# DLRM tower with gathered embeddings: where the upper layers stand in TensorE's order, who adds the row numbers, when the late weights are loaded

## The reference

```
e = stack(tbl_f[ids[:, f]])                        # 2048 x 26 x 64
x = layer_norm(dense @ Wd.T)                       # 2048 x 128
y = layer_norm(e @ Ws.T)                           # 2048 x 26 x 128
y = layer_norm(einsum('bne,pn->bep', y, Wsi))      # 2048 x 128 x 32
T = concat([x, y^T])                               # 33 vectors of 128
Zflat = lower triangle of T @ T^T                  # 528
z = layer_norm(Zflat @ Wl.T) * mask(384)           # 2048 x 512
h = relu([z, dense] @ W_top1 + b1)                 # 512
h = relu(h @ W_top2 + b2)                          # 256
out = h @ W_top3                                   # 2048 x 1
```

## Time and profile before

| What | Value |
| --- | --- |
| median of 3 runs | 572.98 us |
| the profiled execution: span from first to last instruction | 572.2 us |
| TensorE matmuls busy | 509.5 us (89%) |
| VectorE busy | 400.8 us (70%) |
| ScalarE busy | 280.8 us (49%) |
| GpSimd busy | 400.9 us (70%) |
| mean granted TensorE clock | 0.967 |
| gathers, L530 | 416, 398.4 us busy, 958 ns each, 126.8 us idle in front of them |
| y_var, L409 | 64, 1220 ns each |
| projection, L631 | 64 pairs, 662 ns a record |

### The profile page before, as it was taken

The page is one execution under the profiler, slowest core; times in us unless marked ns, Lnnn a source line. Parts: engine busy times, 40 slices in busy tenths (PEclk is TensorE's granted clock), DMA queues, the critical chain, the costliest instruction groups (busy, mean ns, idle before and its releaser), DMA issues.

```text
span 572.2 us, 17022 instructions
## 1 busy us (share of the span) xinstructions
PE 509.5 (89%) x6783; PEld 396.8 (69%) x6783; DVE 400.8 (70%) x707; ACT 280.8 (49%) x727; POOL 400.9 (70%) x423
## 2 busy tenths in 40 slices
PE   1768759899999999999999999999999999898887
PEld 1644438677868677777778687778677777777665
DVE  3747666786778878677878786878878776777720
ACT  0514553454636555455545454646455455545433
POOL 5777777777777777777777777777777777777000
PEclk9958886999999999999999999999999999999999
DMA  7711113131212213131313131222213131313020
GB/s 266 281 28 29 25 29 90 27 91 28 82 38 67 51 33 87 27 93 28 91 28 93 27 91 29 78 41 67 54 39 80 27 90 29 91 27 91 5 65 1
DMA packets 28704, 36.39 MB, mean 64 GB/s; under 512 B 10731, under 2 KB 19379, under 8 KB 28113
## 3 DMA queue, kind: packets, MB, share of 16 engines
q0 software_dynamic: 13408, 13.81, 12.6%
q1 hardware_dynamic: 15218, 21.50, 11.0%
HBM read 26.09 MB, written 9.18 MB: 62 GB/s over the span
## 4 chain that ended last, share of the span: by engine, by line
PE 22%; POOL 22%; DVE 22%; issue 19%; ACT 9%; DMA 4%; SPq 1%; DVEq 0%; ACTq 0%
POOL rows L530 22%; PE bank_z L661 7%; DVE y_var L409 5%; PE bank_d L689 4%; DVE y L399 4%; DVE r_vec L425 4%; PE bank_z L644 4%; ACT y_sq L813 3%; DVE bank_z L417 2%; ACT y_std L819 2%; DMA wsi_b<-in_wsi_b 2%; DVE scaled L364 2%; PE bank_b L631 2%; PE bank_z L604 1%; ACT h L893 1%
## 5 line engine op out<-in xcount | busy, mean ns | idle before, releaser
L530 POOL DMA_INDIRECT rows<-in_table,ids_all x416 | 398.4, 958 | 126.8 <-issue 125.9
L409 DVE TENSOR_REDUCE y_var<-y_sq 128x32 f32<-128x1024 f32 x64 | 78.1, 1220 | 45.3 <-ACT y_sq L813 45.3
L813 ACT ACTIVATE y_sq<-y 128x512 f32<-128x512 f32 x128 | 80.3, 631 | 36.7 <-DVE y L399 36.4
L631 PE MATMUL bank_b<-mixed,gs_row 64*128 64x512 f32 x128 | 74.4, 662 | 19.8 <-ACT mixed L842 19.6
L644 PEld LDWEIGHTS bank_z<-r_vec 128*32 128x32 f32 x4096 | 47.8, 111 | 59.8 <-issue 58.0
L621 PE MATMUL bank_a<-wsi_b,scaled 128*128 128x192 f32 (+3 forms) x512 | 84.0, 309 | 2.1 <-DVE scaled L389 2.0
L425 DVE TENSOR_TENSOR r_vec<-y,bank_z 128x512 f32<-128x512 f32 x128 | 82.3, 684 | 2.2
L621 PEld LDWEIGHTS bank_a<-wsi_b,scaled 128*128 128x128 f32 x512 | 78.2, 195 | 3.2 <-DVE scaled L389 3.2
L661 PE MATMUL bank_z<-wl,zd 128*128 128x512 f32 x160 | 74.7, 614 | 1.2 <-DMA zd<-zx 1.2
L835 ACT ACTIVATE row_std<-row_var,eps 128x8 f32<-128x8 f32 (+1 forms) x64 | 19.2, 300 | 113.6 <-DVE row_var L373 89.3
L631 PE MATMUL bank_c<-mixed,gs_row 64*128 64x512 f32 x128 | 74.4, 662 | 0.0
(11 more groups left out here) (111 smaller groups left out, 609.4 us busy)
## 6 DMA issues: line engine op xcount, KB each, us to landing
zx<-zs SPq DMA_DIRECT2D x15, 560.0 KB, 3.8
rows<-in_table,ids_all POOLq DMA_INDIRECT x416
dense_t<-in_dense_t SPq DMA_DIRECT2D x1, 2048.0 KB, 8.5
wl<-in_wl SPq DMA_DIRECT2D x1, 1280.0 KB
w<-in_w SPq DMA_DIRECT2D x1, 1280.0 KB, 16.3
wsi_b<-in_wsi_b SPq DMA_DIRECT2D x1, 1248.0 KB, 11.5
zd<-zx SPq DMA_DIRECT2D x15, 80.0 KB
zd<-zx SPq DMA_DIRECT2D x15, 70.0 KB
```

What stands on the lines that cost most here:

```text
L409: v.tensor_reduce(y_var[:, k % BANKS, :], y_sq[:, k % 2, :, :].rearrange("e a (s p) -> e (a s) p", p=PROJ), AX_X, ALU.add).then_inc(y_var_ ...
L530: nc.gpsimd.indirect_dma_start(rows[t % 2][:, c, D * blk:D * (blk + 1)], None, io["table"], bass.IndirectOffsetOnAxis(ap=ids_all[:, n:n + ...
L631: pe.matmul(bank_y[blk][:], gs_row[half, :], mixed[half, k % 2, :], start=True, stop=True)\
L813: nc.scalar.activation(y_sq[:, k % 2, blk, :], y[:, k % 2, blk, :], ACT.Square).then_inc(y_squared, 1)
```

## The change

In TensorE's loop `upper(w)` moves from the end of the step to the place between `gram_product(w+1)` and `project(w)`; only `turn_z`, which stood in `upper`, stays at the end of its step. ids and first row numbers come in one load, and VectorE adds them in two pieces (tile 0, then tiles 1 to 15) where GpSimd added them in one; the first gathers wait for the first piece, all later ones for the second. The load of `wl` waits for `prep` at "x_row0", the loads of `w1`, `w2` and `w3` for "end". The masks get a semaphore of their own, and the three users of `wl` (`fold`, `scale_linear`, `last_step_weights`) wait for its load.

```diff
--- before.py
+++ after.py
@@ -110,8 +110,8 @@
         ident = sb("ident", [P, P])
         ones = sb("ones", [P, P])
         eps = sb("eps", [P, 1])
-        ids_all = sb("ids_all", [P, TILES * 2 * CHUNKS], I32)
-        row_base = sb("row_base", [P, 2 * CHUNKS], I32)
+        ids_based = sb("ids_based", [P, (TILES + 1) * 2 * CHUNKS], I32)
+        row_base, ids_all = ids_based[:, 0:2 * CHUNKS], ids_based[:, 2 * CHUNKS:]
         ws_t = sb("ws_t", [P, E])
         gs_row = sb("gs_row", [P, E])
         ws_e = sb("ws_e", [P, P])
@@ -172,8 +172,9 @@
         x_r = sb("x_r", [P, TILES])
         out_row = sb("out_row", [1, B])
 
-        s_ids, s_small, s_wsi, s_wl, s_dense, s_top = (
-            sem(n) for n in ("ids_loaded", "small_loaded", "wsi_loaded", "wl_loaded", "dense_loaded", "top_loaded"))
+        s_ids, s_small, s_wsi, s_masks, s_wl, s_dense, s_top = (
+            sem(n) for n in ("ids_loaded", "small_loaded", "wsi_loaded", "masks_loaded", "wl_loaded", "dense_loaded",
+                             "top_loaded"))
 
         gathered = [[sem(f"gathered_{parity}_{g}") for g in range(len(GROUPS))] for parity in ("even", "odd")]
         ids_ready = sem("ids_ready")
@@ -258,6 +259,16 @@
                 dve.wait_ge(prep, count[0])
 
             v = nc.vector
+
+            def add_row_base(first, end):
+                v.tensor_tensor(ids_all[:, 2 * CHUNKS * first:2 * CHUNKS * end].rearrange("p (t n) -> p t n", t=end - first),
+                                ids_all[:, 2 * CHUNKS * first:2 * CHUNKS * end].rearrange("p (t n) -> p t n", t=end - first),
+                                row_base.rearrange("p (o n) -> p o n", o=1).broadcast_to([P, end - first, 2 * CHUNKS]),
+                                ALU.add).then_inc(ids_ready, 1)
+
+            dve.wait_ge(s_ids, 16)
+            add_row_base(0, 1)
+            add_row_base(1, TILES)
             step(v.memset(eps[:], EPS))
             step(v.memset(ones[:], 1.0), "constants")
             dve.wait_ge(s_small, 16 * 7)
@@ -322,7 +333,7 @@
                 finish_x(j)
 
 
-            dve.wait_ge(s_wl, 16 * 3)
+            dve.wait_ge(s_masks, 16 * 2)
             bq = col["bsi_q"].rearrange("p (t o) -> p t o", o=1)
             fw = fold_w[:, :, 0:64]
             step(v.tensor_tensor(fw, mask_a[:].rearrange("p (o n) -> p o n", o=1).broadcast_to([P, STEPS, 64]),
@@ -334,6 +345,7 @@
 
             def last_step_weights():
 
+                dve.wait_ge(s_wl, 16)
                 dve.wait_ge(fold_done, 1)
                 last = wl[:, 0, :]
                 step(v.tensor_scalar(last, last, col["gsi_q"][:, 0:1], None, ALU.mult))
@@ -472,19 +484,20 @@
 
         @block.sync
         def _(sp):
-            for dst, src in ((ids_all, "ids"), (row_base, "row_base")):
-                sp.dma_start(dst[:], io[src]).then_inc(s_ids, 16)
+            sp.dma_start(ids_based[:], io["ids_based"]).then_inc(s_ids, 16)
             for dst, src in ((ws_t, "ws_t"), (gs_row, "gs_row"), (ident, "ident"), (cols, "cols"),
                              (wd_t, "wd_t"), (wsi_n, "wsi_n"), (bs_row, "bs_row")):
                 sp.dma_start(dst[:], io[src]).then_inc(s_small, 16)
             sp.dma_start(dense_t[:], io["dense_t"]).then_inc(s_dense, 16)
             sp.dma_start(wsi_b[:], io["wsi_b"]).then_inc(s_wsi, 16)
-            for dst, src in ((wl, "wl"), (mask_a, "mask_a"), (mask_b, "mask_b")):
-                sp.dma_start(dst[:], io[src]).then_inc(s_wl, 16)
+            for dst, src in ((mask_a, "mask_a"), (mask_b, "mask_b")):
+                sp.dma_start(dst[:], io[src]).then_inc(s_masks, 16)
+            sp.wait_ge(prep, prep_at["x_row0"])
+            sp.dma_start(wl[:], io["wl"]).then_inc(s_wl, 16)
+            sp.wait_ge(prep, prep_at["end"])
             for dst, src in ((w1, "w1"), (w2, "w2"), (w3, "w3")):
                 sp.dma_start(dst[:], io[src]).then_inc(s_top, 16)
 
-            sp.wait_ge(prep, prep_at["zd"])
             for t in range(TILES - 1):
                 sp.wait_ge(zs_kept, BANKS * (t + 1))
                 if t:
@@ -513,15 +526,12 @@
 
         @block.gpsimd
         def _(pool):
-            pool.wait_ge(s_ids, 32)
-            nc.gpsimd.tensor_tensor(ids_all[:].rearrange("p (t n) -> p t n", t=TILES),
-                                    ids_all[:].rearrange("p (t n) -> p t n", t=TILES),
-                                    row_base[:].rearrange("p (o n) -> p o n", o=1).broadcast_to([P, TILES, 2 * CHUNKS]),
-                                    ALU.add).then_inc(ids_ready, 1)
-            pool.wait_ge(ids_ready, 1)
-
             def gather(k):
                 t, q = divmod(k, BANKS)
+                if k == 0:
+                    pool.wait_ge(ids_ready, 1)
+                if k == 1:
+                    pool.wait_ge(ids_ready, 2)
                 if t >= 2:
                     pool.wait_ge(rows_scaled, k - 2 * BANKS + 1)
                 for c in GROUPS[q]:
@@ -574,6 +584,7 @@
 
             def fold():
 
+                pe.wait_ge(s_wl, 16)
                 for t in range(STEPS):
                     mm = pe.matmul(bank_l[0:65, :], fold_w[:, t, :], wl[:, t, :], start=(t == 0), stop=(t == STEPS - 1))
                 mm.then_inc(fold_done, 1)
@@ -728,7 +739,6 @@
                 if q == 3 and tile >= 1:
                     if tile < TILES - 1:
                         first_dense(tile - 1)
-                        turn_z(tile - 1)
                     else:
                         linear(tile - 1, range(STEPS))
 
@@ -756,6 +766,7 @@
                     mix(w)
                 if ahead:
                     gram_product(w + 1)
+                upper(w)
                 if new:
                     project(w)
                 if old:
@@ -766,7 +777,8 @@
                     fold()
                 if w == 4:
                     fold_bl()
-                upper(w)
+                if w % BANKS == 3 and 1 <= w // BANKS < TILES - 1:
+                    turn_z(w // BANKS - 1)
             end()
 
 
@@ -794,6 +806,7 @@
             def scale_linear(steps):
 
                 if steps[0] == 1:
+                    act.wait_ge(s_wl, 16)
                     act.wait_ge(fold_done, 1)
                 for t in steps:
                     nc.scalar.activation(wl[:, t, :], wl[:, t, :], ACT.Copy, scale=col["gsi_q"][:, t:t + 1],
@@ -1028,8 +1041,8 @@
     ws = np.asarray(x["L0_rec_Ws"])
     arrays = {
         "table": np.concatenate(tables),
-        "ids": ids.reshape(P, -1),
-        "row_base": np.repeat(first_row[feature].T, 2, axis=1).astype(np.int32),
+        "ids_based": np.concatenate([np.repeat(first_row[feature].T, 2, axis=1).astype(np.int32), ids.reshape(P, -1)],
+                                    axis=1),
         "ident": np.eye(P, dtype=f32),
         "ws_t": np.concatenate([ws.T, ws.T]),
         "gs_row": np.broadcast_to(np.asarray(x["L0_rec_gs"]), (P, E)),
```

## The result

The changed kernel took 627.96 us (median of four runs, 626.94 to 628.04), the kernel before 573.35 in the four runs beside it: ratio 1.0944, 95% interval 1.0922 to 1.0967. The forecast was 629.6, in a range of 616 to 642. The profiled execution took 628.0 us and has a span of 626.2.

A forecast was written before the change was run, and what follows sets the result against it. Gathers bound the old kernel, with TensorE close; the new order's loop of waits was to set the time. Its steps reach 598.8, plus 31.0 of tail, less 1.0 at the start, plus 0.8 to the median: 629.6 us, range 616 to 642.

The forecast's parts named there:

- The bound of the old order: Gathers set the old kernel's end at 32.8 us a tile, with TensorE's chain at 30.6 nearly equal.
- The ring: Loop of waits through the engines between successive keep_y(w, 0); with upper products inside, 34.7 us a tile sets the time.
- q = 1: Second of a tile's four steps, q = 0 to 3; its period with second_layer before the projection was forecast at 8.3 us.
- the slack: Spare time in the old loop of waits, which held no upper product; an upper product's full time was to be added.
- The 0.3 us for the copies before the first square: Copies of z and x on ScalarE delay the first square; 0.3 us added to the period after each q = 0 step.
- The start: Before the loop, fewer early loads let wsi_b arrive sooner: gain between nothing and 5.7 us, taken as 1.0.
- a loss of up to 0.5 us: First gather slowed beside VectorE's second addition with two SBUF inputs, losing up to 0.5 of the 1.1 us gained.
- The sum: Step periods added from step 5 at 97.85 put the last keep_y at 598.8; with 31.0 after it, 629.8 us.
- The tail: From the last keep_y to the end: 31.0 us, not shortened by the earlier linear of tile 14.
- (a): Rival: the loop of waits has unseen slack and gathers still set the end, 576 us; chance 0.08.
- (b): Rival: faster, gathers start 1.1 us earlier and stay the bound, 571.9 us; chance 0.04.
- (c): Rival: TensorE's clock falls, its lower level held a tenth of the time, 656 us; chance 0.06.

The follow-up runs named there:

- e7: e1 with first_layer alone moved between gram and projection on TensorE: 589.96 us, ratio 1.024 to the kernel before.
- e1: The changed kernel with TensorE's old order put back, row numbers on VectorE and late weight loads kept: 574.26 us, ratio 0.9964 to the kernel before.
- e11: e1 run once more, unchanged, beside e9 and e10: 573.03 us, ratio 0.9977 to the kernel before.
- e6: e1 with third_layer alone moved between gram and projection on TensorE: 575.11 us, ratio 0.9987 to the kernel before.
- e8: e1 with VectorE's one subtraction over wsi_b cut into six pieces: 572.96 us, ratio 0.9948 to the kernel before.
- e9: e1 with third_layer between gram and projection and VectorE's subtraction over wsi_b in six pieces: 573.23 us, ratio 0.9984 to the kernel before.
- e10: e1 with all weights loaded at the start, so only the row numbers on VectorE remain of the change: 572.97 us, ratio 0.9977 to the kernel before.
- e2: The kernel before with TensorE's new order alone, loads and row numbers as before: 628.49 us, ratio 1.0886 to the kernel before.
- e3: The changed kernel with ScalarE's copy of the turned rows put before the second square: 605.01 us, ratio 1.0503 to the kernel before.
- e5: The changed kernel with the upper products between mix and gram, not between gram and projection: 605.91 us, ratio 1.0523 to the kernel before.
- e4: The changed kernel with linear alone put back at the end of its step: 612.58 us, ratio 1.065 to the kernel before.

## Why the prediction was right, point by point

**The bound of the old order.** Two limits lay close. e7 shows it: 1.3 us a tile more, and the end is TensorE's, no longer the gathers'. e1 and e11 show the other side: TensorE's chain is 5 us ahead at step 7 (108.33 and 108.62) and has no lead left at step 59 (512.86 and 512.41, against 512.97). In the traces of the kernel before and of e1, e6, e8, e9, e10 and e11 the end comes 43.0 to 44.1 us behind the start of the last gather. That spread is about as large as the differences between them, so a shift of the end by a few tenths of a us can't be traced to the gathers.

**The ring.** Right in place and size. Forecast 8.4, 8.3, 10.6 and 7.3; measured 8.29, 7.93 to 8.30, 10.74 and 7.27. e2 shows that the order alone does it, e3 that ScalarE's order closes the ring, e6 and e7 that a piece costs only what is over the slack. The 0.3 us for the copies before the first square shows in q = 1 in one of three or four tiles; I had put it in each. A tile as forecast, 34.7, is 0.2 over the mean of 34.50, 2.6 us over 13 tiles; over an undisturbed tile, 34.3, it is 0.4. The fall of the clock in tile 7, told below, hides some of it.

**The start.** Forecast a gain of 1.0, measured 0.73 at the first transposition. The gathers start 0.87 earlier, forecast 1.1, both within their bounds. The first gather, for which I had a loss of up to 0.5 us beside the second addition, took 1.20 us where it was 1.17. The gain of 0.73, though, compares two traces. The first transposition starts at 32.60 to 33.61, 32.99 on the mean, in the nine with row numbers on VectorE and the subtraction in one piece, and at 33.33 and 33.52 in the two with the old loads: some 0.4 us, less than the traces differ among themselves. The rule of the Trainium skill ("DMA: Bandwidth & Descriptors", section "Queues, rings and completion order") gave half a microsecond less gain than my 1.0; 0.73 lies between, and the means are nearer to it. e10 speaks for the rule: with `wl` and the rest queued behind it `wsi_b` came no later than in e1_loads and e11.

**The sum.** y of step 5 was forecast at 97.85 - 1.0 = 96.85 and came at 96.66; step 7 at 113.8 and 113.41; step 59 at 564.9 and 561.89; step 63 at 597.8 and 594.51. The tail was 31.0 and came as 31.7, and the runs' median lay 1.8 and not 0.8 above the span. The 0.8 was a misreading: I took the span of one execution from the median of others, and in every run the time is 1.8 to 1.9 us over the span of the same run. The errors partly cancel, which is luck: 0.4 too much up to step 7, 2.6 in the 13 tiles and 0.3 in tile 15, against 0.7 and 1.0 too little in the tail and above the span, 1.6 us in all.

**The tail** grew by 0.7, which I had no term for. In the last tile TensorE has nothing to do between the interaction of step 62 and that of step 63. From the changed kernel's timeline of TensorE:

```profile
600.13 1.16 PE L655 MATMUL bank_z<-r_vec 128*32 128x35 f32 x64 [4.95 <-DVE r_vec L437]
601.22 3.78 PE L691 MATMUL bank_a<-dense_t,w 128*128 128x128 f32 x16
...
608.96 4.57 PE L672 MATMUL bank_z<-wl,zd 128*128 128x512 f32 x10
```

After 4.95 us without work the interaction takes 1.16 us and `first_dense` 3.78, where it took 2.05 in the earlier trace rows: the granted clock was 0.50 from 600 to 605. e2_order, with the same order and the same wait of 4.95 us, shows that this is nearly the whole of it: there `first_dense` took 3.10, 0.68 less, and the tail was 30.9. In the kernel before `linear` of tile 14 stood in this gap. `linear` of the last tile then started behind `first_layer`, without a wait for its z, where it had waited 1.16 us for it before.

**What was wrong.** GpSimd did not wait for scaled rows from tile 12: only two gathers, at 245.57 and 522.07, were released by `scale_rows`, and both started after the usual 0.3 us. VectorE waits for the projection at q = 0, 1 and 2 (1.1, 0.9 and 3.7 us), but not at q = 3, where its own work is as long as the ring; I had said 1.5 to 6 us in each step. TensorE waits 0.3 to 1.7 us in front of gram, where I had 0.6 to 1.7. None was a term of the sum.

**The rivals.** (a) and (b) fall with e2. (c), a lower clock, happened in a small way:

```profile
297.85 1.33 PE L621 MATMUL bank_z<-gram,rows_t 128*128 128x128 f32 x6 [1.41 <-ACT rows_t L840]
298.98 3.23 PE L713 MATMUL bank_z<-h,w 128*128 128x128 f32 x16
```

In tile 7 the second layer took 3.23 us, where it takes 1.95 in the other tiles; gram in front of it had waited 1.41 us for the copy. The granted clock was 0.82 from 295 to 300 and 0.84 from 300 to 305, and the period was 9.61 in place of 7.9 to 8.3. It happened once here and twice in e2. That costs 1.3 to 1.7 us each time and not the 26 us that the rival adds to the forecast. What sets it off is open: in tiles 2, 5, 10 and 13 gram had waited longer, 1.70 us, and the second layer behind it took its 1.95.

## What to carry to other kernels

Before moving work into a gap of one engine, write down the ring of waits through all engines that passes the new place, with each engine's own program order as a link, and compare its length with the period: a piece costs nothing up to the slack and its full time above it. Work taken out of the ring is not free either: in e4 `linear` outside it made the next period longer by 2.6 us. Filling a short wait (TensorE's for ScalarE's copy of the mixed rows was 5.3 us of the 244 in the kernel before) isn't worth a place inside the ring. Where two limits lie close, as gathers and TensorE here, a gain on one is small and a loss on the other is large.

## What the runs showed that I had not expected

A gather that starts while VectorE runs the subtraction of 2.76 us, with two SBUF inputs, takes 2.49 to 3.48 us for 0.944 in all eleven traces that have it in one piece, and each ended 0.81 or 0.82 us after that instruction. Cut in six pieces of 0.59 us it no longer does (1.05 at most). Beside the reduction just in front of it, 2.75 us with one SBUF input, the two gathers that started in the changed kernel took 0.94 us each. The Trainium skill ("GPSIMD Engine Reference", section "1. Specifications") names the shared way to SBUF; the trace agrees. But removing the 2.4 us did not shorten the stream by as much: the time from the first gather to the last was 524.8 us in e1_loads, 524.4 in e11 and 523.7 in e8 and e9. The later gathers of 1.0 to 1.47 us, show the same pattern. In the changed kernel:

```profile
217.33 0.69 DVE L401 TENSOR_TENSOR scaled<-rows,row_r 128x512 f32<-128x512 f32 x1
217.48 1.36 POOL L540 DMA_INDIRECT rows<-in_table,ids_based  x1 [0.30 <-issue]
```

`scale_rows` has two SBUF inputs too; the gather starts 0.15 us after it and ends 0.82 us after its end. Over the thirteen traces 198 gathers later than 26 us took 1.0 us or more. In 189 of them `scale_rows` was running when the gather started, and the gather ended 0.80 to 0.83 us after it; the other nine lie beside VectorE's preparation. Where the two started within 0.05 us of each other, 38 times, the gather took its 0.94 or 0.95. The time over 0.944 us, added up, is 2.8 us in e3 and 8.6 in e5, and what is left of the stream is 518 or 519 us (within 0.1) in every trace: so the stream's length (521.8 to 526.6) hangs on how often a gather happens to start beside `scale_rows`. No run moved or split `scale_rows` to test this, so the cause is read from the traces alone, and what such an edit would give is not shown.
